# Probabilities as the stationary side of the way through V, the scaling moved behind it, four ring banks, and a second attention net without loops

## The reference, cut to what matters

```python
qkv = x @ Wqkv                      # x token-shifted, 128 -> 3 * heads * 64
q, k = rotary(l2norm(q) * qs), rotary(l2norm(k) * ksc)
sim  = einsum('bhwid,bhwjd->bhwij', bq, bk2) * QK_SCALE   # own window and the one before
sim  = where(mask, -max, sim)
attn = softmax(sim, -1)
out  = einsum('bhwij,bhwjd->bhwid', attn, bv2)
x    = x + out @ Wo
x    = x + (a * gelu(gate)) @ W2 + b2   # a, gate = split(layernorm(shift(x)) @ W1 + b1)
```

## Time and profile before

| | |
|---|---|
| median of 3 runs | 8505.15 us (8498.15 to 8508.95) |
| the profiled execution | 8497.0 us, span 8495.2 us |
| mean granted TensorE clock | 0.91 |
| busy over the span | PE 80%, DVE 66%, ACT 59%, POOL 49% |
| first local-attention net | about 700 to 4700 us of the span |
| second local-attention net | about 5750 to 6750 us |

### The profile page before, as it was taken

The page is one execution under the profiler, slowest core; times in us unless marked ns, Lnnn a source line. Parts: engine busy times, 40 slices in busy tenths (PEclk is TensorE's granted clock), DMA queues, the critical chain, the costliest instruction groups (busy, mean ns, idle before and its releaser), DMA issues. The chain is left out here.

```text
span 8495.2 us, 245223 instructions
## 1 busy us (share of the span) xinstructions
PE 6835.2 (80%) x92628; PEld 4785.2 (56%) x92628; DVE 5632.5 (66%) x11929; ACT 4981.5 (59%) x10706; POOL 4196.7 (49%) x3732
## 2 busy tenths in 40 slices
PE   5777999999999999999999499997888567634267
PEld 2325666666666666666666388884555323323245
DVE  6895776777677677777677367666667578845432
ACT  4545777777777777777777344436767555302122
POOL 4555665666566666666566144454444355430000
PEclk8888999999999999999999699998989788866578
DMA  3321111111111111111111200000000133331001
GB/s 125 124 94 52 41 38 51 39 41 49 40 38 52 41 38 48 42 40 46 44 40 40 70 5 5 5 5 24 14 21 15 44 122 124 112 101 59 21 0 30
DMA packets 234082, 412.19 MB, mean 49 GB/s; under 512 B 41944, under 2 KB 125360, under 8 KB 214128
## 3 DMA queue, kind: packets, MB, share of 16 engines
q1 hardware_dynamic: 225344, 377.76, 14.1%
q10 hardware_dynamic: 1584, 15.21, 0.4%
q0 software_dynamic: 6144, 5.25, 0.4%
HBM read 208.61 MB, written 32.18 MB: 28 GB/s over the span
## 5 line engine op out<-in xcount | busy, mean ns | idle before, releaser
L763 POOL TENSOR_TENSOR L0f_qr<-L0f_qs,L0f_table 128x512 f32<-128x512 f32 x776 | 989.2, 1275 | 459.5 <-ACT L0f_qs L804 357.0
L1018 PE MATMUL L0f_ring<-L0f_wqkv,L0f_hT 128*128 128x512 f32 x2324 | 1173.4, 611 | 42.2 <-ACT L0f_hT L799 37.5
L770 POOL TENSOR_TENSOR L0f_qr<-L0f_qr,L0f_m 128x512 f32<-128x512 f32 x776 | 984.7, 1269 | 163.7 <-issue 106.4
L834 ACT ACTIVATE L0f_scores<-L0f_scores,L0f_nmx,L0f_rn 128x64 f32<-128x64 f32 x3072 | 982.6, 400 | 131.4 <-DVE L0f_nmx L939 130.3
L1075 PEld LDWEIGHTS L0f_o<-L0f_pT,L0f_vmix 64*64 64x64 f32 x18480 | 759.3, 136 | 159.1 <-issue 136.5
L1075 PE MATMUL L0f_o<-L0f_pT,L0f_vmix 64*64 64x32 f32 x18480 | 801.8, 221 | 49.8 <-ACT L0f_pT L842 32.0
L1075 PE MATMUL L0f_o<-L0f_pT,L0f_vb 64*64 64x32 f32 x6160 | 750.8, 221 | 1.2 <-issue 1.0
L777 POOL TENSOR_TENSOR L0f_qr<-L0f_qr,L0f_rn 128x512 f32<-128x512 f32 x388 | 396.3, 1042 | 687.7 <-DVE L0f_rn L931 686.4
L908 DVE TENSOR_TENSOR L0f_m<-L0f_ring,L0f_table 128x512 f32<-128x512 f32 x776 | 524.2, 685 | 254.4 <-ACT L0f_qs L804 245.8
L1075 PEld LDWEIGHTS L0f_o<-L0f_pT,L0f_vb 64*64 64x64 f32 x6160 | 604.3, 137 | 2.0 <-issue 2.0
L916 DVE TENSOR_REDUCE L0f_ssq<-L0f_sq 128x8 f32<-128x512 f32 x776 | 509.7, 676 | 76.8 <-ACT L0f_sq L809 71.9
(11 more groups left out here) (538 smaller groups left out, 17156.5 us busy)
## 6 DMA issues: line engine op xcount, KB each, us to landing
L0f_vmix<-L0f_vb SPq DMA_DIRECT2D x768, 128.0 KB, 2.4
L0a_bc_all<-L0a_bc_rows SPq DMA_DIRECT2D x32, 2048.0 KB, 11.5
L2a_bc_all<-L2a_bc_rows SPq DMA_DIRECT2D x32, 2048.0 KB, 11.6
L0f_vmix<-L0f_vb SPq DMA_DIRECT2D x672, 64.0 KB, 2.0
L1f_vmix<-L1f_vb SPq DMA_DIRECT2D x96, 128.0 KB, 2.3
L0f_wqkv<-L_ffn_wqkv_dram SPq DMA_DIRECT2D x7, 1536.0 KB, 6.3
L2f_parts<-L2f_zero ACTq DMA_DIRECT2D x8, 1088.0 KB, 11.4
n_s<-mixer_out SPq DMA_DIRECT2D x32, 256.0 KB, 5.0
```

The source lines that it names most:

```text
L763: e.tensor_tensor(rotated, qs[:, q % QN], spread(cos, 1, 8), ALU.mult).then_inc(cosed.sem, 1)
L770: e.tensor_tensor(rotated, rotated, m2[:, q % SN], ALU.add).then_inc(added.sem, 1)
L834: a = e.activation(s_ps[:, s, h, j], s_ps[:, s, h, j], ACT.Exp, bias=nmx[:, s, col:col + 1], scale=rn[:, tt, 2 * u, col:col + 1])
L1018: e.matmul(bank[:], hT[:, tt * P:tt * P + P], wqkv[:, layer % 2, col:col + 512], start=True, stop=True).then_inc(full, 1)
```

## The change

In the first net:
- the value matmuls take pT as the stationary side (32 columns) and V as the moving one (64 columns). The result has tokens on the partitions and lies in two banks, one for each half.
- the exps write `prob` in SBUF; the flip reads it unscaled. The sums and reciprocals are kept (two buffers). A new VectorE event `onorm` scales the value's result by them into `o_sb`, a new TensorE step `oflip` transposes it, and `ocopy` reads that.
- the scores have one buffer of two banks in place of two; the value result takes two banks in place of one, and the ring has four banks in place of three.
- `ORDER`, `SIDE`, `TOOK` and `LATER` have new entries.

In the second net the loops over layers and sequences are written out, `wqkv` and `scales` get two halves, the next layer's load is issued a layer ahead, and the load at the end of the last layer is left out.

```diff
-    ORDER = [("side", 0), ("score", 0), ("value", 1), ("v", 1), ("out", 0), ("side", 1), ("v", 0), ("k", 0), ("q", 0),
-             ("tk", 0), ("score", 1), ("tq", 0), ("flip", 0), ("q", 1), ("side", 2), ("value", 0), ("tk", 1), ("k", 1),
-             ("tq", 1), ("flip", 1)]
-    SIDE = [(("fshift",), (0, 1)), (("fturn",), (0, 2)), (("gate", 0), (1, 0)), (("gate", 1), (1, 0)),
-            (("gate", 2), (1, 0)), (("fetch",), (1, 2)), (("up", 0), (1, 1)), (("layer",), (2, 1)), (("shift",), (2, 1)),
-            (("up", 1), (1, 2)), (("up", 2), (2, 2)), (("down",), (3, 2))]
+    ORDER = [("side", 0), ("value", 1), ("score", 0), ("v", 0), ("oflip", 1), ("v", 1), ("out", 0), ("side", 1), ("tq", 0),
+             ("flip", 0), ("q", 0), ("tk", 0), ("k", 0), ("score", 1), ("value", 0), ("q", 1), ("tk", 1), ("side", 2),
+             ("k", 1), ("oflip", 0), ("flip", 1), ("tq", 1)]
+    SIDE = [(("fshift",), (0, 1)), (("fturn",), (0, 2)), (("gate", 0), (1, 0)), (("gate", 1), (1, 0)), (("gate", 2), (1, 0)),
+            (("fetch",), (0, 2)), (("up", 0), (1, 1)), (("layer",), (2, 1)), (("shift",), (2, 1)), (("up", 1), (2, 0)),
+            (("up", 2), (3, 0)), (("down",), (3, 2))]
...
+        if kind == "value":
+            return [(D["onorm"], ("onorm",) + step[1:])]
...
+    LATER = {"exp": 1.71, "exp_gap": 0, "unflip": 0, "ocopy": 0, "xn": 2.39, "act_ring": 0, "copy": 0, "square": 0.97,
+             "ssq": 4.53, "rot": 2.83, "newton": 8.28, "max": 1.62, "norm": 5.57, "dve_ring": 0.89, "cos": 5.2, "add": 5.49,
+             "kmul": 7.11, "rstd": 4.29, "onorm": 1.07}
...
-        n_ring = 3
+        n_ring = 4
...
-        both_ps = r.ps("scores", [P, 2, 2, 512])
...
-        o_ps = r.ps("o", [P, GP, P])
+        score_ps = r.ps("scores", [P, 2, 512])
...
+        value_ps = r.ps("o", [P, 2, 512])
...
+                                e.wait_ge(*totaled(it, key, 2))
+                                e.wait_ge(*flipped(it, key, 2))
...
-                            a = e.activation(s_ps[:, s, h, j], s_ps[:, s, h, j], ACT.Exp, bias=nmx[:, s, col:col + 1],
+                            a = e.activation(prob[:, s, j, h], s_ps[:, h, j], ACT.Exp, bias=nmx[:, s, col:col + 1],
...
-                            e.tensor_reduce(sums[:], s_ps[:, s], AX.X, ALU.add)
+                            e.tensor_reduce(sums[:, s], prob[:, s], AX.X, ALU.add).then_inc(totaled.sem, 1)
...
-                            e.tensor_tensor(prob[:, s].rearrange("p j (h k) -> p h j k", h=2), s_ps[:, s], spread(sums[:], 3, KEYS),
-                                            ALU.mult).then_inc(scaled.sem, 1)
+                        elif kind == "onorm":
+                            key = step[1:]
+                            s = parity(key)
+                            e.wait_ge(*oflipped(it, key, 1))
+                            e.wait_ge(*valued(it, key))
+                            e.tensor_tensor(o_sb.rearrange("p j h d -> p h j d"), o_ps,
+                                            spread(sums[:, s].rearrange("p j h -> p h j"), 3, DH), ALU.mult).then_inc(oscaled.sem, 1)
...
-                            e.wait_ge(*unflipped(it, key, 2))
+                            e.wait_ge(*unflipped(it, key, 1))
...
-                            e.wait_ge(*scaled(it, key))
+                            e.wait_ge(*exped(it, key))
...
-                                        a = e.matmul(o_ps[half, j, cols], values, pT[half, s, j, cols], start=True, stop=True)
+                                        a = e.matmul(o_ps[cols, h, j], pT[half, s, j, cols], values, start=True, stop=True)
                             a.then_inc(valued.sem, 1)
+                        elif kind == "oflip":
+                            key = step[1:]
+                            e.wait_ge(*oscaled(it, key))
+                            for j in range(GP):
+                                a = e.transpose(ot_ps[:, j // 2, j % 2], o_sb[:, j], g.ident[:])
+                            a.then_inc(oflipped.sem, 1)
...
-        wqkv = r.sb("wqkv", [P, 3 * inner])
+        wqkv = r.sb("wqkv", [P, 2, 3 * inner])
...
-                with e.Fori(0, depth) as l:
-                    with e.Fori(0, BATCH - 1) as b:
-                        body(e, l * BATCH + b, b, l, False)
-                    body(e, l * BATCH + BATCH - 1, BATCH - 1, l, True)
+                for l in range(depth):
+                    for b in range(BATCH):
+                        body(e, l * BATCH + b, b, l, b == BATCH - 1)
...
+                load_qkv(1)
...
-                    load_qkv(bass.ds((l + 1) % depth, 1))
+                    if l < depth - 1:
+                        for done in ring.all_written(last, [s for s in uses if s[0] == "proj" and s[1] == TT - 1]):
+                            e.wait_ge(*done)
+                            e.sem_inc(passed, 1)
+                        load_qkv((l + 2) % depth)
```

More of the change, by code:

```diff
@@ L397, in tile_steps @@
                 steps += [("out", prev)]
-            elif (what, i) == ("value", last_u):
-                steps += [("value", prev, i)]
+            elif what in ("value", "oflip") and i == last_u:
+                steps += [(what, prev, i)]
             else:
@@ L408, in narrow_attention_net @@
               [turn(0, what, c) for c in range(n_chunks) for what in "qk"] + [proj(0, "v", c) for c in range(n_chunks)])
-    AFTER = [("value", TT - 1, last_u), ("out", TT - 1)] + FEED
+    AFTER = [("value", TT - 1, last_u), ("oflip", TT - 1, last_u), ("out", TT - 1)] + FEED
     def lag(step):
@@ L420, in lag @@
             return -1 if step[1] == 0 else 0
-        if kind in ("value", "ocopy"):
+        if kind in ("value", "oflip", "ocopy"):
             return 1 if step[1:] == (TT - 1, last_u) else 0
@@ L437, in sequence @@
         return b if lag(step) == 0 else (b - lag(step)) % BATCH
-    TOOK = {"score": 1.5, "value": 1.3, "flip": 1.0, "turn": 0.6, "proj": 0.95, "out": 0.25 * pairs, "shift": 1.5, "fshift": 1.0,
+    TOOK = {"score": 1.1, "value": 0.8, "flip": 0.45, "oflip": 0.45, "turn": 0.6, "proj": 0.95, "out": 0.25 * pairs, "shift": 1.5, "fshift": 1.0,
             "fturn": 0.6, "gate": 0.95, "up": 0.95, "down": 2.8, "fetch": 0.0, "layer": 0.0, "end": 0.0}
@@ L462, in act_events @@
             return [(D["unflip"], ("unflip",) + step[1:])]
-        if kind == "value":
+        if kind == "oflip":
             return [(D["ocopy"], ("ocopy",) + step[1:])]
@@ L500, in narrow_attention_net @@
              3.0, "max": 0.2, "norm": 5.0, "norm_gap": 2.0, "unflip_dve": 0.5, "dve_ring": 0.3, "cos": 1.0, "add": 2.5,
[L501 to L504, removed]
+             "kmul": 6.0, "rstd": 2.0, "onorm": 0.3}
+    LATER = {"exp": 1.71, "exp_gap": 0, "unflip": 0, "ocopy": 0, "xn": 2.39, "act_ring": 0, "copy": 0, "square": 0.97,
+             "ssq": 4.53, "rot": 2.83, "newton": 8.28, "max": 1.62, "norm": 5.57, "dve_ring": 0.89, "cos": 5.2, "add": 5.49,
+             "kmul": 7.11, "rstd": 4.29, "onorm": 1.07}
     RING = ("shift", "proj", "turn", "out", "fshift", "fturn", "gate", "up", "down")
@@ L600, in programs @@
             valued = r.count("valued", made_by(STEPS, "value"))
-            ocopied = r.count("ocopied", made_by(STEPS, "value"))
+            oscaled = r.count("oscaled", made_by(DVE_STEPS, "onorm"))
+            oflipped = r.count("oflipped", made_by(STEPS, "oflip"))
+            ocopied = r.count("ocopied", made_by(ACT_STEPS, "ocopy"))
             fed = [s for s in STEPS if s == ("down",)]
@@ L877, in _ @@
                 if STEPS is BEFORE:
-                    e.memset(o_ps[:], 0.0)
+                    e.memset(value_ps[:], 0.0)
                 def body(e, it, b, l, last):
@@ L1043, in body @@
                                         half = slice(h * DH, h * DH + DH)
-                                        a = e.matmul(s_ps[rows, s, h, j], qT[half, tt % 2, GP * u + j, rows],
+                                        a = e.matmul(s_ps[rows, h, j], qT[half, tt % 2, GP * u + j, rows],
                                                      kT[half, GP * u + j, cols], start=False, stop=j == GP - 1)
@@ L1482, in mix_all @@
                         mix(it, tt)
-                with e.Fori(0, depth) as l:
-                    one = bass.ds(l, 1)
+                for l in range(depth):
+                    one = slice(l, l + 1)
                     first, last = l * BATCH, l * BATCH + BATCH - 1
@@ L1501, in _ @@
                     e.dma_start(ln[:], w["ln"][one].rearrange("o p a -> p (o a)")).then_inc(feed_ready, 16)
-                    with e.Fori(1, BATCH - 1) as b:
+                    for b in range(1, BATCH - 1):
                         mix_all(first + b)
                     mix_all(last)
-                    for done in ring.all_written(last, [s for s in uses if s[0] == "proj" and s[1] == TT - 1]):
-                        e.wait_ge(*done)
-                        e.sem_inc(passed, 1)
-                    load_qkv(bass.ds((l + 1) % depth, 1))
+                    if l < depth - 1:
```

(4 more changed lines are left out.)

43 lines of the change are left out of this document (23 added, 20 removed).

## The result

The changed kernel takes 8575.96 us (median of 4 runs, 8573.46 to 8581.23) against 8507.05 us of the kernel before on the same chip (8498.15 to 8515.05): ratio 1.008, 95% interval 1.0068 to 1.0092. It is slower by 0.8%, some 69 us; the forecast was 8440 us, with a range from 8240 to 8570. The profiled execution has a span of 8573.4 us, 78.2 more than before.

The account below looks back on a forecast made before the run. TensorE was taken to bound the first net, waits to decide the second. 8497.0 - 36 (first net) - 30 (second net) = 8431 us profiled; the median of runs lies 8.15 above: 8440 us, range 8240 to 8570.

Parts of the forecast that it names:

- Value step: First net, TensorE: a value step takes 0.80 us instead of 1.99, the added oflip 0.43; 292 us less work.
- Walk of the tiles: First net, step-by-step timing of a sequence's four tiles with their waits: 81.0 us against 81.74, 36 us less over 48 sequences.
- The term that isn't in the sum: First net: only TensorE's work gets shorter, by 292 us, of which 256 turn into waits for the other engines.
- Clock: Rival, chance 0.24: the 3.8 us gap in each tile 0 brings half clock on TensorE, 58 us more, 8498 us.
- Unflip behind the copies: Rival, chance 0.17: negated max and exps start 1.05 us later a tile, delaying unflip: 8640 us, at half size 8540.
- Other engines: First net, ScalarE's exps into SBUF and VectorE's scaling and sum: change taken as 0, bounds 46 ns either way.
- Second net: Written-out loops save 21 us in 16 sequences, with the layer-end load 30 us; bounds 9 and 60.

Follow-up runs that it names:

- the shifted pair: Changed kernel plus 35 counting instructions a sequence, with 22 or 101 more ahead of the first sequence: 8845.46 us (1.0414) and 8638.13 us (1.0175).
- the first run with transposes: Changed kernel plus 16 identity transposes, results unread, ahead of the wait of oflip(3,1): 8570.85 us against 8503.16 before, ratio 1.0079.
- three of the orders tried above: Changed kernel with score ahead of value: 1.0692; that with newton(1) behind onorm(3,1): 1.0427; newton so moved and a whole new TensorE order: 1.0277.
- its own run: Kernel before with only the second net written out, first net as before: 8481.57 us against 8493.02, ratio 0.9988.

## Why the prediction was wrong

**Value step** (0.80 us, oflip 0.43): right, 0.79 and 0.44. The Trainium skill's floor of about 25 ns from start to start ("TensorE: Matmul & The Clock Gate", "Wait — 56ns, not 53.3ns?") would have made it 1.6; 64 matmuls in 0.79 us, 12.3 ns each, contradict it again; they are walked over the array's halves and 32-column strips.

**Walk of the tiles** (T1 18.7, T2 19.3, T3 17.9, T0 25.1, 81.0 together): the tiles without a stall and wholly at full clock have medians of 18.8, 19.4, 18.1 and 24.5 (24, 25, 15 and 8 tiles), 80.8 together. All tiles have medians of 18.81, 19.42, 19.37 and 26.30. The waits were the right ones, in the right order: oflip(3,1) waits behind newton(1), but it starts 5.8 us into tile 0 on average (6.55 forecast), for a gap of 2.3 (3.8); value(1) waits for pT, 70.3 us. Tile 0's length was met better (24.5 against 25.1) than the gap in it, which is in part luck. The forecast for the first net, -36 us, is the walk's.

**The term that isn't in the sum**: "So only TensorE's work gets shorter, and the question is what the new order waits for." This step failed. Between the waits of the walk TensorE was taken to run its steps at their row's length, and the arrival of its program was put at nothing. But a value step at 0.79 us beside a score at 1.10 runs through 262 instructions in 1.9 us, and the program comes in blocks of 256; at a stall, 2.2 to 3.1 us lie between the start of the block's DMA and the block's first instruction. The stalls are 107.8 us, against 6.9 before, when the same pair took 3.1 us; the shifted pair shows where they come from. The same step left TensorE's clock out of the sum (below). Of the 292 us that were to leave TensorE's work 104 did, and its idle time rose by 194, of which 101 are stalls, where 256 were forecast. The Trainium skill ("Runtime: NRT & Kernel Launch", "Instruction fetch mechanics") has the blocks, 16 KiB or 256 instructions, and calls the cost of crossing one "mostly hidden"; the size agrees with the packet of 16384 bytes and the distance of 256, "hidden" doesn't hold for these steps (107.8 us of stalls).

**Clock** (a rival, 0.24, +58 us): its mechanism happened, 47 stretches and 133 us more at half clock, most of it caused by the gap in tile 0, as the first run with transposes shows (222 us down to 116). At 0.24 us per us it costs 32 us, with the interval above 8 to 56.

The first net came out 126 us above its forecast (+90.1 against -36). The stalls explain some 70 to 80 of it by their place, 101 at most at their full length; the clock 32, give or take 24. The two are the most of the 126; how it divides between them is estimated, not shown, and by these sizes some 20 us are left open.

**Unflip behind the copies** (0.17, 8540 to 8640): the time fell into its range for another reason. The negated max takes 393 ns, not 620, and the tiles without a stall at full clock are those of the walk. Its premise, that ScalarE's list is what every tile runs into, came true in three of the orders tried above.

**Other engines** (0 for the new sides): right. The exp into SBUF lasts 417 ns against 400, but in both kernels the next one starts 0.289 us behind it, and four in a row take 1.29 us in either. The walk's own figure was too small: 1.15 us for four, where its row shows 1.29, and 2.3 for eight, where eight take 2.47, on the chain to flip, which waits 33.1 us.

**Second net** (-30, bounds 9 and 60): -23.4 in the trace, -11 as its own run (0.9979 to 0.9997). The wait for the scales at a layer's end is gone. The wait of fshift fell from 31.8 us to 19.7, 0.7 us a sequence where 0.5 was forecast; inside the body, where 0.8 was forecast, little was won, and the flip's wait for its probabilities rose from 21.1 to 35.0 us. Waits after:

```profile
PE L1f_ring L1907 <- DVE f L1759: 19.7, 17, 1.6
...
PE L1f_ring L1821 <- DVE f L1759: 15.1, 31, 1.0
```

## What to carry to other kernels

Making a step of many small instructions faster can cost a good part of what it gains: count instructions beside microseconds. Gaps with no releaser at instruction numbers that are equal modulo 256 are the sign that a block runs out in less time than the next takes to arrive. A long instruction between two such steps takes the gaps away (107.8 to 18.9 us), but it pays only if nothing waits for the step that it delays: here it cost 38 us alone and gained 43 beside newton. Where the order of the engines' lists is written out, find the entry that stands last in one body and ahead of a new step in the next: moving newton(1) by one place gained 93 us, more than the whole change lost. And a score, copy or exp that is made ready earlier helps only if nothing that is more urgent stands behind it on the same engine.

## What was not expected of the hardware

The same program with 79 more counting instructions at its start ran 207 us faster. Semaphore instructions on TensorE that nobody waits for follow each other at 0.151 us, where a small matmul starts every 12.3 ns.
